# Re-ordering the ramp of a cross-attention and ternary feed-forward kernel: w1's sum and rounding first, context ahead of w2, one batch's attention rows between two first layers

## The reference, cut to what matters

```python
# x (4, 2048, 512), ctx (4, 154, 512)
# attention: mask j % 2048 == i, with 154 context rows. A row i < 154 sees context row i alone;
# a row i >= 154 has nothing unmasked, and its softmax is uniform: the mean of v
x = x + (where(i < 154, ctx[i], mean(ctx)) @ Wv) @ Wout + bout
h = layernorm(layernorm(x)) * gamma + beta
hq = clip(round(h * 127 / max|h|), -128, 127)            # per row
w1q = clip(round(w1 / mean|w1|), -1, 1)                  # one mean over the whole matrix
g = gelu((hq @ w1q.T) / scales + b1)                     # 2048 wide
gq = clip(round(g * 127 / max|g|), -128, 127)
w2q = clip(round(w2 / mean|w2|), -1, 1)
out = x + (gq @ w2q.T) / scales + b2
```

## Time and profile before

| | us |
|---|---|
| runs of the kernel before | 540.47, 538.56, 542.25 (median 540.47) |
| the profiled execution, its own time | 540.51 |
| its span | 538.7 |
| TensorE busy | 527.3 (98%) |
| VectorE busy | 453.6 (84%) |
| ScalarE busy | 435.9 (81%) |
| GpSimd busy | 407.3 (76%) |

### The profile page before, as it was taken

The page is one execution under the profiler, slowest core; times in us unless marked ns, Lnnn a source line. Parts: engine busy times, 40 slices in busy tenths (PEclk is TensorE's granted clock), DMA queues, the critical chain, the costliest instruction groups (busy, mean ns, idle before and its releaser), DMA issues.

```text
span 538.7 us, 8129 instructions
## 1 busy us (share of the span) xinstructions
PE 527.3 (98%) x2434; PEld 227.4 (42%) x2434; DVE 453.6 (84%) x758; ACT 435.9 (81%) x444; POOL 407.3 (76%) x533
## 2 busy tenths in 40 slices
PE   9979989999999999999999999999999999999997
PEld 5433434444444444444444444444444444444443
DVE  3877999999989899988888887988888889887653
ACT  3558899888887888888888888888888889887762
POOL 2288687999998888888888988888888888873300
PEclk9987999999999999999999999999999999999999
DMA  8999233886565656555665556665455574535433
GB/s 310 402 387 294 69 69 102 170 208 162 135 122 141 131 148 119 129 125 130 131 143 142 123 129 117 141 132 132 124 123 130 129 142 103 92 86 100 95 78 98
DMA packets 137015, 78.72 MB, mean 146 GB/s; under 512 B 114246, under 2 KB 114310, under 8 KB 136972
## 3 DMA queue, kind: packets, MB, share of 16 engines
q1 hardware_dynamic: 135636, 75.80, 57.3%
q10 hardware_dynamic: 1335, 2.41, 1.3%
HBM read 33.88 MB, written 17.05 MB: 95 GB/s over the span
## 4 chain that ended last, share of the span: by engine, by line
PE 95%; DVE 3%; POOL 1%; ACT 1%; issue 1%; POOLq 0%; DVEq 0%; ACTq 0%
PE py L1055 41%; PE p L1040 28%; PE pab L1040 14%; PE p L983 3%; PE p L1030 3%; PE pab L1008 2%; PE pab L1030 1%; POOL xr L387 1%; PE pab L968 1%; DVE hx L792 1%; PE py L1016 1%; PE py L1008 1%; DVE w2q L779 1%; ACT hid L578 0%; PE py L974 0%
## 5 line engine op out<-in xcount | busy, mean ns | idle before, releaser
L1055 PE MATMUL py<-w2q,hqT 128*128 128x512 bf16 x1024 | 231.0, 379 | 1.7 <-DVE hqT L829 1.7
L587 ACT ACTIVATE hq<-hid,hscale 128x2048 int8<-128x2048 f32 x64 | 128.1, 2002 | 46.2 <-DVE hscale L821 46.2
L1040 PE MATMUL p<-w1q,xqT 128*128 128x512 bf16 x688 | 159.4, 380 | 0.0
L1055 PEld LDWEIGHTS py<-w2q,hqT 128*128 128x128 bf16 x1024 | 100.1, 98 | 123.0 <-DVE hqT L829 2.7
L578 ACT ACTIVATE hid<-p,xdeq 128x1024 f32<-128x1024 f32 x86 | 95.0, 1106 | 15.9 <-PE p L1040 11.2
L1040 PEld LDWEIGHTS p<-w1q,xqT 128*128 128x128 bf16 x688 | 63.8, 98 | 81.2 <-issue 10.1
L387 POOL TENSOR_TENSOR xr<-xr,attn 128x512 f32<-128x512 f32 x64 | 83.3, 1320 | 18.7 <-DVE attn L727 17.2
L402 POOL TENSOR_TENSOR hx<-hx,beta_b 128x512 f32<-128x512 f32 x64 | 91.7, 1454 | 4.4 <-ACT hx L563 4.3
L815 DVE TENSOR_REDUCE hmax<-hid 128x1 f32<-128x1025 f32 x64 | 78.1, 1220 | 18.0 <-ACT hid L578 17.4
L406 POOL TENSOR_TENSOR xr<-xr,b_b 128x512 f32<-128x512 f32 x64 | 92.6, 1465 | 0.0
L809 DVE TENSOR_REDUCE hid<-hid 128x1 f32<-128x1024 f32 x64 | 77.4, 1209 | 8.8 <-ACT hid L578 8.8
(11 more groups left out here) (88 smaller groups left out, 408.9 us busy)
## 6 DMA issues: line engine op xcount, KB each, us to landing
xr<-x SPq DMA_DIRECT2D x64, 256.0 KB, 2.9
out<-xr SPq DMA_DIRECT2D x64, 256.0 KB, 2.4
raw<-w1T SPq DMA_DIRECT2D x8, 512.0 KB, 12.2
hid<-wvT SPq DMA_DIRECT2D x8, 256.0 KB, 7.8
wout<-wout_d ACTq DMA_DIRECT2D x8, 256.0 KB, 8.7
wout<-w2T SPq DMA_DIRECT2D x3, 512.0 KB, 5.5
xr<-w2T SPq DMA_DIRECT2D x2, 512.0 KB, 11.1
attn<-ctxm_d SPq DMA_DIRECT2D x4, 256.0 KB, 8.1
```

Source lines behind the costliest of these rows:

```text
L587: nc.scalar.activation(hq8[:, t % 2, :], hid[:, t % 2, 0:HID], ACT.Copy, scale=col(hscale, t))\
L1040: mm = nc.tensor.matmul(hidden_bank(t, n), xT[:, k, :], w1q[:, k, n * D:(n + 1) * D], start=False, stop=(k == KD - 1))
L1055: mm = nc.tensor.matmul(py[:, t % 2, :], hqT[:, t % 2, c // 2, c % 2, :], w2q[:, c, :], start=(c == 0), stop=(c == 2 * NJ - 1))
```

## The change

Nothing is added or taken away but waits: every call stays, in another order, and `out_rows` waits for the copied products one by one (`wvo_copied, k + 1` inside its loop) instead of for all four ahead of it.

```diff
--- before.py
+++ after.py
@@ -290,36 +290,36 @@
             load_w1(6)
             load_w1(7)
             load_x(4)
+            load_ctx()
             load_w2(0)
             load_b1_rows()
             load_x(5)
             load_w2(1)
-            load_ctx()
             load_w2(2)
+            transpose_x(0)
             load_x(6)
             load_w2(3)
             load_w2(4)
-            transpose_x(0)
+            transpose_x(1)
             load_w2(5)
             load_w2(6)
             load_w2(7)
             load_x(7)
             load_x(8)
             load_x(9)
+            transpose_x(2)
+            transpose_x(3)
             sp.dma_start(b2_b[:, 0, :], b2.partition_broadcast(P)).then_inc(b2_loaded, 16)
             load_x(10)
-            transpose_x(1)
             load_x(11)
             load_x(12)
             load_x(13)
-            transpose_x(2)
-            transpose_x(3)
+            transpose_h(0)
+            load_x(14)
+            load_x(15)
+            transpose_h(1)
             transpose_x(4)
-            transpose_h(0)
             transpose_x(5)
-            load_x(14)
-            transpose_h(1)
-            load_x(15)
             transpose_h(2)
             sp.wait_ge(tail_copied, 1)
             sp.dma_start(tail_rows, tail_out).then_inc(tail_stored, 16)
@@ -440,37 +440,37 @@
             pool.wait_ge(mean_copied, 1)
             add_attention(0, 1)
             add_attention(1, 1)
-            add_attention(2, 1)
-            add_attention(3, 1)
             pool.wait_ge(const_set, 3)
             inverse_std(0, 1)
+            add_attention(2, 1)
             inverse_std(1, 1)
             pool.wait_ge(beta_loaded, 16)
             add_beta(0, 1)
+            add_attention(3, 1)
+            add_beta(1, 1)
             inverse_std(2, 2)
-            add_attention(4, 1)
-            add_beta(1, 1)
-            add_attention(5, 1)
             widen_x(0, 1)
             pool.wait_ge(wscale_done[0], 1)
             scale_rows(0, 1)
+            widen_x(1, 1)
+            scale_rows(1, 1)
             add_beta(2, 1)
             add_beta(3, 1)
+            add_attention(4, 1)
+            scale_rows(2, 2)
+            add_attention(5, 1)
+            add_attention(6, 1)
+            widen_x(2, 2)
             inverse_std(4, 2)
-            scale_rows(1, 1)
-            add_attention(6, 1)
-            widen_x(1, 1)
+            add_attention(7, 1)
             add_beta(4, 1)
             add_beta(5, 1)
-            scale_rows(2, 2)
-            widen_x(2, 2)
-            add_attention(7, 1)
             add_attention(8, 1)
             scale_rows(4, 2)
             add_attention(9, 1)
+            inverse_std(6, 2)
             pool.wait_ge(b2_loaded, 16)
             add_b2(0)
-            inverse_std(6, 2)
             add_attention(10, 1)
             add_attention(11, 1)
             widen_x(4, 2)
@@ -613,52 +613,52 @@
             abs_w1(3)
             times_std(0)
             abs_w1(5)
-            copy_wvo(2)
             times_std(1)
             abs_w1(6)
+            copy_wvo(2)
+            round_x(0)
             abs_w1(7)
-            round_x(0)
             times_std(2)
             times_std(3)
+            round_x(1)
             abs_w2(0)
             copy_wvo(3)
             round_weights(0, 1)
             round_weights(0, 3)
             abs_w2(1)
+            gelu(0, 0)
+            gelu(0, 1)
+            abs_w2(2)
+            abs_w2(3)
+            round_x(2)
+            round_x(3)
+            abs_w2(4)
+            gelu(1, 0)
+            abs_w2(5)
+            gelu(1, 1)
+            abs_w2(6)
+            abs_w2(7)
             times_std(4)
             times_std(5)
-            round_x(1)
-            abs_w2(2)
-            abs_w2(4)
-            abs_w2(3)
-            abs_w2(5)
-            abs_w2(6)
-            abs_w2(7)
-            gelu(0, 0)
-            round_x(2)
-            gelu(0, 1)
-            round_x(3)
             round_weights(1, 0)
             round_weights(1, 1)
+            round_h(0)
+            round_weights(1, 2)
+            gelu(2, 0)
+            round_weights(1, 3)
+            gelu(2, 1)
+            round_h(1)
+            round_weights(1, 4)
             round_x(4)
             round_x(5)
-            gelu(1, 0)
-            gelu(1, 1)
-            round_h(0)
-            round_weights(1, 2)
-            round_weights(1, 3)
-            round_weights(1, 4)
-            gelu(2, 0)
-            times_std(6)
-            gelu(2, 1)
-            round_h(1)
             round_weights(1, 5)
+            widen_h(0)
             round_weights(1, 6)
-            widen_h(0)
             round_weights(1, 7)
-            times_std(7)
             gelu(3, 0)
             gelu(3, 1)
+            times_std(6)
+            times_std(7)
             round_h(2)
             widen_h(1)
             gelu(4, 0)
@@ -865,57 +865,57 @@
             dve.wait_ge(gamma_loaded, 16)
             centre(0)
             statistics(1)
+            centre(1)
+            abs_w1(4)
             statistics(2)
+            centre(2)
             statistics(3)
-            abs_w1(4)
-            centre(1)
-            centre(2)
+            centre(3)
             x_scale(0, 1)
-            centre(3)
-            statistics(4)
             weight_sum(0)
-            centre(4)
+            x_scale(1, 1)
             weight_scale(0)
-            statistics(5)
-            x_scale(1, 1)
+            round_w1(0)
+            clip(0, 0)
+            clip(0, 1)
+            round_w1(2)
+            clip(0, 2)
+            clip(0, 3)
+            x_scale(2, 2)
             ctx_sum(0)
             ctx_sum(1)
             ctx_sum(2)
-            centre(5)
-            x_scale(2, 2)
             attn_rows(0)
             ctx_sum(3)
-            round_w1(0)
-            round_w1(2)
-            clip(0, 0)
-            clip(0, 1)
-            clip(0, 2)
-            clip(0, 3)
+            half_scale(0)
+            statistics(4)
+            centre(4)
+            hidden_scale(0)
+            ctx_means()
+            statistics(5)
+            centre(5)
+            half_scale(1)
             attn_rows(1)
+            hidden_scale(1)
+            weight_sum(1)
             attn_rows(2)
-            weight_sum(1)
-            ctx_means()
             weight_scale(1)
-            x_scale(4, 2)
-            half_scale(0)
             statistics(6)
             statistics(7)
-            hidden_scale(0)
-            half_scale(1)
+            x_scale(4, 2)
+            centre(6)
+            tail_rows_out()
+            clip(1, 0)
+            clip(1, 1)
             statistics(8)
             statistics(9)
-            hidden_scale(1)
-            centre(6)
-            centre(7)
             half_scale(2)
-            attn_rows(3)
-            tail_rows_out()
-            hidden_scale(2)
-            clip(1, 0)
-            clip(1, 1)
             clip(1, 2)
             clip(1, 3)
+            centre(7)
+            hidden_scale(2)
             widen_h(0)
+            attn_rows(3)
             clip(1, 4)
             clip(1, 5)
             clip(1, 6)
@@ -998,13 +998,13 @@
 
             def out_rows(i):
                 b = (i + 1) % B
-                pe.wait_ge(wvo_copied, KD)
                 if i == 2:
                     pe.wait_ge(attn_copied, 1)
                 if i == 3:
                     pe.wait_ge(wmean_done[1], 1)
                 pe.wait_ge(ctxm_loaded, 16 * KD)
                 for k in range(KD):
+                    pe.wait_ge(wvo_copied, k + 1)
                     mm = nc.tensor.matmul(row_banks[i], ctxm[k][:, b * P:(b + 1) * P], wvo[:, k, :],
                                           start=(k == 0), stop=(k == KD - 1))
                 mm.then_inc(attn_done, 1)
@@ -1065,20 +1065,20 @@
             weight_total(0)
             products(30, 32)
             out_rows(0)
-            out_rows(1)
             bias(0)
-            out_rows(2)
             first_layer(0, 0)
             first_layer(0, 1)
-            weight_total(1)
+            out_rows(1)
             bias(1)
             first_layer(1, 0)
             first_layer(1, 1)
-            out_rows(3)
+            out_rows(2)
+            weight_total(1)
+            tail_product()
             bias(2)
             first_layer(2, 0)
             first_layer(2, 1)
-            tail_product()
+            out_rows(3)
             bias(3)
             first_layer(3, 0)
             first_layer(3, 1)

```

## The result

The median of six runs is 545.34 us (543.57 to 546.96), that of the kernel before beside it 539.89 us (538.56 to 542.25). The ratio is 1.0093, with a 95% interval of 1.0067 to 1.0119: 5.4 us slower, where 539.3 had been forecast. The profiled execution took 544.44 us, its span is 542.6, and what lies around the span is 1.8 us as before (540.51 against 538.7).

A forecast was written before the change was run, and what follows sets the result against it. TensorE was taken as the bound, with only the ramp's 11.5 us to win: 0.8 + 0.7 + 1.2 + 1.7 and some 1.3 of clock back, 3.5 + 1 paid anew, so 1.2 gained: 540.5 to 539.3 us (8 in 10: 536.0 to 542.7).

The forecast's parts named there:

- w1's sum: First matmul with ones, waiting for abs_w1(7) behind round_x(0): starts at 36.85 against 37.66, 0.8 of the 3.5 us stop gained.
- Per-k waits, context ahead: At out_rows(0): the 0.69 us stop goes; ctxm's earlier load by itself is worth nothing; out_rows(0) ends at 44.5 to 46.5.
- w1's rounding: VectorE idles about 3 us (3.1) ahead of clip(0, 1), until 43.6; first_layer(0) ends at 49.3.
- tile 3's 1.25: A 1.25 us idle of VectorE for tile 3, counted in the 6.55 us of its idle time after the change.
- The second sum: weight_sum(1) on VectorE put at 63.5, range 62.3 to 64.7; TensorE stops 3.5 us at weight_total(1), range 2.3 to 4.7.
- the prediction's own rival: The first clock fall, at w1's sum, doesn't come: weight_sum(1) at 61.8, total 537.6 us; chance 0.12.
- the rival with 0.27: A second fall of the clock, at weight_total(1): gelu(2, 0) and ScalarE 2.2 us later, total 541.5 us; chance 0.27.
- The step that failed: Ramp's end: last w2 rounding at 81.1, clip 0.4, second half of second_layer(0) 1.75: done at 83.2 against 84.4.
- T: Time of weight_sum(1), 63.5; gelu(2, 0) can start at T + 6.3, w2's last rounding ends at T + 17.6.
- the first fall that the forecast counted in: Clock falls again in w1's sum's stop and returns at 41 to 44; some 1.3 us of the clock come back.
- moving rows between first layers: One batch's out_rows between first layers: no work taken away, 10.7 us of it cover gelu(0, 1)'s 1.18 us stop.
- x tile 6, held behind `transpose_x(0)`: SyncE's list: seven loads start up to 9 us later; GpSimd adds to tile 6 only at 53; cost nothing.

The follow-up runs named there:

- e1: Changed kernel with weight_sum(1) right behind half_scale(1) and weight_scale(1) ahead of hidden_scale(1) on VectorE: 546.92 us (1.0148).
- e5: Changed kernel with three stops filled: unused products ahead of the first weight_total, out_rows(2) and the first half of second_layer(0) done twice: 542.32 us (1.0044).
- e6: Kernel before with three unused fp32 matmuls filling the stop ahead of the first weight_total: 538.45 us (0.9979).
- e15: e13 with out_rows(1) back ahead of bias(0), in place of the two filling matmuls there: 541.92 us (1.0047).
- e13: e9 with stops filled by unused matmuls ahead of bias(0) and second_layer(0), and the latter's first half done twice: 539.63 us (1.0008).
- e2: Changed kernel with the matmuls of out_rows(2) done twice, filling the stop at weight_total(1): 545.81 us (1.0098).
- e3: Changed kernel with GpSimd's additions of b2 for tiles 1 to 3 moved behind add_beta(7): 548.11 us (1.0162).
- e7: Changed kernel with out_rows(1) back ahead of bias(0), nothing else undone: 544.29 us (1.0094).
- e8: Changed kernel with b2 added to only 8 of 512 columns of tiles 1 to 3: 544.41 us (1.0095).
- e12: Changed kernel with the context loads back behind w2's second block: 546.25 us (1.0116).
- e14: Changed kernel, VectorE's list alone reordered: ready work ahead of clip(0, 1), x_scale(2, 2) behind the context sums; round_x(0) left: 544.88 us (1.0090).
- e4: Changed kernel with round_x(0) back behind abs_w1(7) on ScalarE: 543.80 us (1.0082).
- e9: Changed kernel with both the ScalarE edit of e4 and the VectorE edits of e14: 540.14 us (1.0007).

## Why the prediction was wrong, step by step

*w1's sum.* Forecast for the first matmul with ones (L995): 36.4 to 37.2. It started at 38.12, 1.3 us later than the 36.85 of the sum; 0.7 of it is a stop at 7.5 us on a load of `wout`, ahead of all that was changed. The wait of VectorE for `abs_w1(7)` is 1.9, as in the working. The stop is 3.01 and not 2.65, and the clock stayed full in this execution.

*Per-k waits, context ahead.* No stop stands ahead of `out_rows(0)`, as forecast. Not seen: 1.62 us ahead of `bias(0)`. `transpose_x(0)` was put at 39.2 and issued at 42.03. Of these 2.8 us 1.3 are the late sum, and the others `scale_rows(0)`, which took 2.7 us beside VectorE's rounding and 1.2 before. Two of its rows:

```profile
39.43 1.17 POOL L416 TENSOR_TENSOR rr<-xscale,wscale 128x1 f32<-128x1 f32 x1
40.67 0.66 POOL L419 TENSOR_TENSOR rr<-rr 128x1 f32<-128x1 f32 x1
```

These take 0.19 each in the kernel before. That the two engines hold each other up had been weighed for the long instructions only. TensorE would not have stopped there at a low clock, which the prediction took for granted: it had `out_rows(0)` end at 44.5 to 46.5, and it ended at 43.7.

*w1's rounding.* `clip(0, 1)` waited 1.87 where 3.1 had been worked out with a low clock; `x_scale(2, 2)`, not forecast, waited 1.23; tile 3's 1.25 didn't come. `first_layer(0)` ended at 49.2 (49.3).

*The second sum.* `weight_sum(1)` at 63.27 (63.5), stop 3.50 (3.5): right, but by luck. Inside it the late start (1.3) and the shorter wait at `clip(0, 1)` (1.2) cancelled, and the clock had stayed full at the first stop, for which the prediction's own rival had 61.8. The clock fell at the second stop, which was the rival with 0.27, priced at 2.2; the tail product took 1.8 more. `widen_h(0)` ended at 80.4 (80.1).

*The step that failed* is the last: "Its clip adds 0.4, and the second half of `second_layer(0)` 1.75: 83.2". It priced one clip behind ScalarE's last rounding and left out what VectorE's own list has in front of that clip. VectorE was done with `widen_h(0)` in time (80.4) and went on without a wait through `attn_rows(3)` and four clips at 1.01 us, until 85.0, where 81.5 had been forecast: 3.5 us. The stop that this made, 2.45 us, took the clock with it, another 1.6: the second half took 3.4 us to its next row, where 1.75 had been priced. That is 5.1 of the 5.3 us between 83.2 and 88.5, and nearly the whole distance from the 539.3 forecast to the 544.44 of the profiled execution. At the 1.43 us of before the four clips would have ended at 82.4, ahead of ScalarE's last rounding. That was done at 82.8, 1.7 behind its 81.1, because the fall of the clock held up `gelu(2, 0)` (at T + 8.1 and not T + 6.3; the rest took 11.4, as worked out). So the 3.5 us stand for two things that the sum did not have: 1.7 the clock would have cost by way of ScalarE in any case, and 1.8 are the clips' pace beside the additions of b2. e1, where ScalarE is done at 78.3 and the clips still end at 85.1, shows that an earlier ScalarE alone would have gained nothing.

*The base of the comparison* hid the sign. The gain of 1.2 us was counted against an execution that had lost 2.2 to the clock (540.5 against 538.3 at full clock), and VectorE's idleness after against 5.9 us, of which 2.6 was that clock's doing. Against 3.0 at full clock, the new order's 7.0 are 4 us more, which is what e5 and e6 measured. The rival "a second fall of the clock" ended at 541.5: its mechanism came true, but with two low stretches behind later stops and not one, without the first fall that the forecast counted in, and on top of a schedule that was itself longer.

*Right as far as it went:* moving rows between first layers moves no work, and what it covers is there (e15 against e13), but only for a kernel whose VectorE keeps up. Loading the context early is worth nothing that could be measured. x tile 6, held behind `transpose_x(0)`, was issued 12.5 us later than before (44.27 against 31.73) and not 9, and no engine is seen waiting for it: that cost was rightly put at nothing.

## What to carry to other kernels

Where two engines have little slack, a re-ordering is to be priced by the idle time that it puts into the list of the engine that sets the end: here three waits of 1.2 to 1.9 us on VectorE came back as 2.9 to 3.9 us. Before a profile serves as the base of such a sum, take out the waits that a low clock in that execution made; filling the stops with unused matmuls, in both kernels, separates schedule from clock, if the runs that kept the clock are compared. And at the end of the chain, count all that stands ahead of the last instruction on each engine, not only the releaser of the last wait.

## What the runs showed of the hardware

The clock fell behind shorter stops than the 3.50 us from which the prediction argued, and not always behind longer ones. The same stop of 3.01 to 3.04 us ahead of the first matmul with ones left the clock full in the profiled executions of after, e1 and e2 (the four products behind it took 1.96 us) and was followed by a low clock in those of e3, e7, e8, e12 and e14 (2.58 to 3.76 us). In e4 and e9, behind stops of 1.86 and 1.93 us ahead of `bias(0)`, sixteen (fifteen recorded) matmuls of `first_layer(0)` took 5.41 and 4.96 instead of 3.63. The stop of 2.45 us ahead of the second half of `second_layer(0)` cost the clock in the kernel after and in e4, and not in e12. In e9, TensorE:

```profile
44.86 0.39 PE L1030 MATMUL p<-b1rows,xqT 32*128 32x512 bf16 x4 [1.93 <-DMA xqT<-xq]
45.54 4.96 PE L1040 MATMUL p<-w1q,xqT 128*128 128x512 bf16 x15 [0.28 <-issue]
```

The same program had different mean granted clocks in different executions, and each 0.001 is about 0.5 us: e1 took 543.3 at 0.996 and 548.2 and 549.7 at 0.984 (5.6 us in twelve steps), e9 537.2 to 538.8 at 1.000 and 544.4 to 545.6 at 0.987. What decides at a given stop, in a given execution, stays open. So does how the schedule's part would divide between the three waits taken one at a time; the runs show only that the two edits together take them away.
